# The routed stage, the step sizes and the mixer's first projections put into one block

## The reference, cut to what matters

```python
x = _layernorm(x + _L0_ffn_ref(x, ...))     # routed LoRA: base + top-2 of 8 experts of rank 16
x = _layernorm(x + _L1_attn_ref(x, ...))    # mixer: 8 groups of 16 heads, head size 64, state 128
# inside _L1_attn_ref
proj = jnp.einsum('bsd,ed->bse', x, in_proj_w)          # gate, heads' inputs, B, C and dt
hBC = jax.nn.silu(conv(hBC))                            # causal convolution, 4 taps per channel
dt = jnp.clip(jax.nn.softplus(dt + dt_bias), 0.0, 100.0)
A_dt = dt * A                                           # A = -exp(A_log)
L = jnp.exp(_segsum(A_dt))                              # decay between two tokens of a chunk
Y_diag = einsum(C, B, L, hs * dt)                       # one chunk of 128 tokens is one batch here
g = (Y + hs * D) * silu(gate)                           # then an RMS norm per group, and out_proj
```

## Time and profile before

| | |
|---|---|
| median of 3 runs | 2599.43 us (2597.91 to 2603.35) |
| the profiled execution's own time | 2601.73 us |
| its span | 2600.0 us |
| PE busy | 2485.4 us, 96% |
| DVE busy | 1861.0 us, 72% |
| ACT busy | 1125.2 us, 43% |
| POOL busy | 1077.5 us, 41% |
| mean granted clock of PE | 0.98 |

### The profile page before, as it was taken

How to read it: one execution, slowest core, us unless ns; L and a number is a source line. 1 busy time by engine, 2 the same in 40 slices (tenths; PEclk the granted TensorE clock), 3 DMA queues, 4 the chain that set the end, 5 groups by cost and what they waited for, 6 DMA issues and landing times. The chain is left out here.

```text
span 2600.0 us, 39171 instructions
## 1 busy us (share of the span) xinstructions
PE 2485.4 (96%) x14056; PEld 2038.8 (78%) x14056; DVE 1861.0 (72%) x2531; ACT 1125.2 (43%) x2660; POOL 1077.5 (41%) x889
## 2 busy tenths in 40 slices
PE   7878599999999999999999999989999999999999
PEld 4436488888888888888888888778888888888886
DVE  4865488697786986967859869656666666666675
ACT  2321334334343443343434433445556556565551
POOL 3011264555555546655555556633223223122223
PEclk9988799999999999999999999989999999999999
DMA  4000242131221321313213213111001001010100
GB/s 155 1 1 9 73 145 91 53 146 37 105 102 37 138 89 57 142 37 114 94 48 127 89 61 110 57 37 38 25 17 42 17 25 41 10 33 25 55 3 33
DMA packets 61555, 163.83 MB, mean 63 GB/s; under 512 B 8336, under 2 KB 8976, under 8 KB 52944
## 3 DMA queue, kind: packets, MB, share of 16 engines
q1 hardware_dynamic: 60144, 159.21, 17.8%
q10 hardware_dynamic: 1248, 2.36, 0.3%
HBM read 158.92 MB, written 2.62 MB: 62 GB/s over the span
## 5 line engine op out<-in xcount | busy, mean ns | idle before, releaser
L267 PE MATMUL pair<-XH,d_w_hi 128*128 128x512 f32 x1160 | 475.4, 410 | 29.1 <-POOL d_w_lo L1332 10.4
L268 PE MATMUL pair<-XL,d_w_hi 128*128 128x512 f32 x1160 | 463.0, 399 | 0.0
L269 PE MATMUL pair<-XH,d_w_lo 128*128 128x512 f32 x1160 | 462.4, 399 | 0.0
L1449 DVE TENSOR_TENSOR_SCAN d_decay<-d_decay,m_delta 128x1024 f32<-128x1024 f32 x128 | 359.9, 2813 | 13.7 <-DMA d_decay<-token_decays 12.3
L1351 POOL TENSOR_TENSOR d_decay<-d_decay,d_cb 128x1024 f32<-128x1024 f32 x128 | 309.6, 2419 | 136.4 <-DVE d_decay L1449 125.5
L1332 POOL TENSOR_TENSOR d_w_lo<-d_w,d_w_hi 128x512 fp32r<-128x512 f32 x144 | 187.9, 1308 | 284.2 <-ACT d_w_hi L1214 283.6
L267 PEld LDWEIGHTS pair<-XH,d_w_hi 128*128 128x128 f32 x1160 | 220.8, 190 | 87.9 <-issue 20.7
L1434 DVE SCALAR_TENSOR_TENSOR d_hs<-pair,d_conv,d_hs 128x1016 f32<-128x1016 f32 (+2 forms) x192 | 242.9, 1265 | 33.1 <-ACT d_hs L1239 28.6
L269 PEld LDWEIGHTS pair<-XH,d_w_lo 128*128 128x128 f32 x1160 | 220.4, 190 | 53.7
L268 PEld LDWEIGHTS pair<-XL,d_w_hi 128*128 128x128 f32 x1160 | 221.1, 191 | 47.6
L1356 POOL TENSOR_TENSOR d_gated_lo<-d_gated,d_gated_hi 128x512 fp32r<-128x512 f32 x128 | 173.6, 1359 | 157.4 <-ACT d_gated_hi L1258 157.4
(11 more groups left out here) (280 smaller groups left out, 6032.7 us busy)
## 6 DMA issues: line engine op xcount, KB each, us to landing
d_decay<-token_decays SPq DMA_DIRECT2D x64, 1024.0 KB, 4.9
d_w<-in_L_w_groups SPq DMA_DIRECT2D x144, 256.0 KB, 2.7
e_w<-in_L_w_heads SPq DMA_DIRECT2D x80, 256.0 KB, 2.7
d_wo<-in_L_wo_groups SPq DMA_DIRECT2D x64, 256.0 KB, 5.0
X<-in_x SPq DMA_DIRECT2D x8, 256.0 KB, 10.4
b_ctx<-in_ctx SPq DMA_DIRECT2D x8, 256.0 KB, 11.8
e_ctx<-in_ctx_t SPq DMA_DIRECT2D x4, 512.0 KB, 6.7
out<-X SPq DMA_DIRECT2D x8, 256.0 KB, 2.0
```

The costliest lines, as they stand in the source:

```text
L267: pe.matmul(out, wh, xh, start=first, stop=False)
L268: pe.matmul(out, wh, xl, start=False, stop=False)
L269: return pe.matmul(out, wl, xh, start=False, stop=last)
L1449: v.tensor_tensor_scan(r, r, m["DELTA"][:], 0.0, ALU.mult, ALU.add).then_inc(q["decay"], 1)
```

## The change

The three stages become one block, `stage_routed_mixer`. The operations of the routed stage and of the step sizes become methods of two classes, `RoutedLora` (low, out, turn on PE; exp, mid_turned, hi on ACT; route, sums, lo on DVE) and `TokenSteps`, and are written between the mixer's own. The barrier and clearing between the stages go, and so does the barrier behind the counters' start values: a semaphore `preset` stands for it. The three splits w_lo of the first weights (0, 1, 2) and that of dt's weight stand on POOL between the norms of batches 1 to 5; the latter was on DVE. dt's temporary tiles lie at the place of the mixer's gated and output-weight tiles, the routed small tiles and three tiles of the autocorrelation in the area of the decays, dt's weights in that of the heads. Methods that are not shown here hold the statements of the functions before, word for word but for names.

```diff
+class TokenSteps:
...
+    def inputs(self, sp):
+        q, a = self.q, self.a
+        sp.dma_start(self.W[:], a["L1_w_dt"].rearrange("p (k n) -> p k n", k=KD)).then_inc(q["in_"], 16)
+        sp.dma_start(self.BIAS[:], a["L1_attn_dt_bias"].rearrange("(p o) -> p o", o=1)).then_inc(q["in_"], 16)
+        sp.dma_start(self.A[:], a["L1_attn_A_log"].rearrange("(p o) -> p o", o=1)).then_inc(q["in_"], 16)
+        sp.dma_start(self.m["PAR"][:], a["L1_params"]).then_inc(q["par_in"], 16)
+
+    def store(self, sp):
+        sp.wait_ge(self.q["cut"], 1)
+        sp.dma_start(self.rows, self.N[:]).then_inc(self.q["stored"], 16)
+        sp.wait_ge(self.q["stored"], 16)
+
+    def project(self, pe, h, routed):
+
+        c = self.c
+        if h == 0:
+            pe.wait_ge(self.q["w_lo"], 1)
+        pe.wait_ge(routed.s.summed, NB - 1 + h)
+        pe.wait_ge(routed.s.lo, 4 * h + 4)
...
+    def w_lo(self, pool):
+        pool.wait_ge(self.q["w_hi"], 1)
+        pool.tensor_tensor(self.WL[:], self.W[:], self.WH[:].bitcast(F32), ALU.subtract).then_inc(self.q["w_lo"], 1)
...
+                for handle in q.values():
+                    sp.sem_inc(handle, START)
+                sp.sem_inc(preset, 1)
+                steps.inputs(sp)
                 for i in range(5):
                     weight(0, i)
+                steps.store(sp)
                 decays(0, 0)
...
                     for j in range(JT - 1):
                         project(g, hs_item(j + 1))
                         turn_hs(g, j)
-                        project(g, gate_item(j))
+                        if g or j:
+                            project(g, gate_item(j))
                         scan(g, j)
...
-                project(0, 0)
+                routed.low(pe, 0)
+                for b in range(NB):
+                    if b + 1 < NB:
+                        routed.low(pe, b + 1)
+                    routed.out(pe, b)
+                    if b:
+                        routed.turn(pe, b - 1)
+                pe.wait_ge(preset, 1)
+                steps.project(pe, 0, routed)
+                routed.turn(pe, NB - 1)
+                project(0, 0, (0,))
+                steps.project(pe, 1, routed)
+                project(0, 0, (1,))
                 project(0, 1)
                 project(0, 2)
+                steps.turn(pe)
+                project(0, gate_item(0))
                 cb(0)
...
-                for i in range(3):
-                    w_hi(0, i)
-                evac(0, 0)
+                routed.exp(act, 0)
+                for b in range(NB):
+                    if b + 1 < NB:
+                        routed.exp(act, b + 1)
+                    routed.mid_turned(act, b)
+                    if b:
+                        routed.hi(act, b - 1)
+                    if b == 1:
+                        steps.w_hi(act)
+                        steps.rates(act)
+                        act.wait_ge(preset, 1)
+                    if b in (2, 3, 4):
+                        w_hi(0, b - 2)
+                routed.hi(act, NB - 1)
+                evac(0, 0, (0,))
+                steps.exp(act)
+                evac(0, 0, (1,))
                 w_hi(0, 3)
-                silu(0, 0)
+                steps.log(act)
                 evac(0, 1)
                 w_hi(0, 4)
+                steps.decay(act)
+                evac(0, 2)
+                silu(0, 0)
                 silu(0, 1)
-                evac(0, 2)
                 silu(0, 2)
...
-                for i in range(5):
-                    w_lo(0, i)
+                pool.memset(routed.L[:], NEG).then_inc(routed.q["const"], 1)
+                steps.constants(pool)
+                for b in range(NB):
+                    if b == 2:
+                        steps.w_lo(pool)
+                        pool.wait_ge(preset, 1)
+                    if b in (3, 4, 5):
+                        w_lo(0, b - 3)
+                    norm_rstd(c, pool, routed.s, b)
+                w_lo(0, 3)
+                w_lo(0, 4)
+                steps.cut(pool)
                 scores(0, 0, 0)
                 scores(0, 0, 1)
...
-                tables(0)
-                skip_table(0)
+                v.wait_ge(routed.q["const"], 1)
+                routed.route(v, 0)
+                for b in range(NB):
+                    if b:
+                        norm_apply(c, v, routed.s, b - 1)
+                    if b + 1 < NB:
+                        routed.route(v, b + 1)
+                    routed.sums(v, b)
+                    if b >= 2:
+                        routed.lo(v, b - 2)
+                    if b == 3:
+                        v.wait_ge(preset, 1)
+                        v.wait_ge(steps.q["par_in"], 16)
+                        conv_table(0)
+                        skip_table(0)
+                        v.wait_ge(q["conv_par"], START + 1)
+                norm_apply(c, v, routed.s, NB - 1)
+                routed.lo(v, NB - 2)
+                routed.lo(v, NB - 1)
+                steps.biased(v, 0)
+                conv(0, 0, (0,))
+                steps.biased(v, 1)
+                steps.one(v)
+                conv(0, 0, (1,))
+                steps.rest(v)
+                steps.steps(v)
+                conv(0, 1, (0,))
+                steps.copied(v)
+                conv(0, 1, (1,))
+                v.wait_ge(steps.q["copied"], 2)
+                token_table(0)
+                conv(0, 2)
+                v.wait_ge(steps.q["mask"], 2)
+                cb_mask(0)
+                v.wait_ge(steps.q["delta"], 1)
                 decay(0, 0, 0)
                 decay(0, 0, 1)
-                for i in range(3):
-                    conv(0, i)
-                cb_mask(0)
+                v.wait_ge(q["tok_par"], START + 1)
```

More of the change, by code:

```diff
@@ L730, in routed_weights @@
                 B=sb("c_b", [P, D]), base_t=base_t, router_lora_a=router_lora_a, lora_b=lora_b)
[L733 to L837, removed]
-                                    WD[:, b, :].rearrange("p (e o) -> p e o", o=1).broadcast_to([P, E0, R0]),
-                                    ALU.mult).then_inc(q["mid"], 1)
-                v.wait_ge(q["const"], 1)
-                route(0)
[L842 to L846, removed]
-                    v.wait_ge(q["out_ready"], b + 1)
-                    v.tensor_tensor(c.X[:, b, :], c.X[:, b, :], c.bank[2 + b % 2][:, :], ALU.add).then_inc(s.summed, 1)
-                    norm_moments(c, v, s, b)
-                    if b >= 2:
-                        turned_lo(c, v, s, b - 2, x_bank(b - 2))
-                norm_apply(c, v, s, NB - 1)
-                turned_lo(c, v, s, NB - 2, x_bank(NB - 2))
-                turned_lo(c, v, s, NB - 1, x_bank(NB - 1))
@@ L963, in stage_mixer, with stage_routed_mixer @@
+def stage_routed_mixer(c, w, m, w_groups, wo_groups, rows, e, a, low):
     nc = c.nc
@@ L973, in stage_mixer, with over @@
         BC = R[:, BC_SLOT, :, :]
+        routed = RoutedLora(c, e, w)
+        steps = TokenSteps(c, m, e, low, a, rows.rearrange("g j (e t) -> (g j e) t", e=2))
+        def over(name, shape, words, dt=F32):
+            return nc.alloc_sbuf_tensor_at(name, shape, dt, offset=low + 4 * words)
         XDT = sb("d_xdt", [P, NB, P])
         SQ, SQS = XDT, sb("d_sq_sum", [P, 2, S])
-        GT = sb("d_gated", [P, JT, T])
+        GT = over("d_gated", [P, JT, T], 0)
         GH, GL = sb("d_gated_hi", [P, 2, 4, S], F32R), sb("d_gated_lo", [P, 2, 4, S], F32R)
-        WOR = sb("d_wo", [P, 2, D])
-        WOH, WOL = sb("d_wo_hi", [P, JT, D], F32R), sb("d_wo_lo", [P, JT, D], F32R)
+        WOR = over("d_wo", [P, 2, D], JT * T)
+        WOH, WOL = over("d_wo_hi", [P, JT, D], JT * T + 2 * D, F32R), sb("d_wo_lo", [P, JT, D], F32R)
         DTG = sb("d_dtg", [P, NB, HG])
@@ L1105, in project @@
                         pe.wait_ge(q["tap"], START + 3 * (g * NU + last_unit + 1))
-                    for h in range(2):
+                    for h in halves:
                         for k in range(KD):
```

342 lines of the change are left out of this document (215 added, 127 removed).

## The result

The changed kernel took 2564.43 us (median of 4 runs, 2563.57 to 2565.1) against 2600.49 (4 runs, 2597.91 to 2603.35) of the kernel before, measured beside it: ratio 0.9858, 95% interval 0.9843 to 0.9872. That is 36.1 us less, where 42.7 were forecast; 2564.43 lies 1.4 above the upper end of the range given (2563).

A forecast was written before the change was run, and what follows sets the result against it. PE's waits in the 94 us between routed batches and mixer were taken as where time could be had. Weight 5's projection 45.2 us earlier, less 2.5 clock penalty, gave 42.7 net: median 2599.43 to 2556.7, range 2550 to 2563.

The forecast's parts named there:

- Ahead of 245.07, at nothing: Routed stretch before batch 7's turn: added splits and copies fit idle time and cost nothing; uncovered, 5.2 us.
- rival 3: Routed stretch grows by up to 5.2 us as splits or copies hold a norm, DVE and PE: 2562; chance 0.11.
- The chain from 245.07 to weight 5's projection: From batch 7's turn through dt, taps, scans and xdt: PE may project weight 5 at 290.4, 45.2 us less.
- The clock penalty of 2.5: Projection behind PE's wait for xdt runs at the lower clock, costing 2.5 us, leaving 42.7 net.
- The 12.3 leaves 0.6: PE's waits for dt between routed batches and mixer, 12.3 us before, shrink to some 0.6.
- the 2.82 is filled: PE's wait for the last norm, before batch 7's turn, is filled by dt's first projection half, 2.86 us.
- the 10.4 and the 8.2 go whole: PE's waits for the first split weight, 10.4 us, and for dt's split weight, 8.2, disappear entirely.
- 1.0 for the split of weight 4 beside dt's steps: POOL's split of weight 4 running beside DVE's dt steps lengthens those by 1.0 us, between 0 and 1.3.
- Rival 2: Memory path ends last: decay rows land late, sharing transfers with two weights; some 3 us, 2560; chance 0.12.
- rival 4: First weights not split in time, PE still waits the 10.4 us at B: 2567; chance 0.04.
- From weight 5's projection on, as before: From there PE works without a hole before and after, so the mixer's loop carries the earlier start to the end.
- Rival 5: Slower: the loop becomes DVE's, each of 64 pairs longer; at 0.75 us per pair 2605; chance 0.02.

The follow-up runs named there:

- e1_mid: Changed kernel with each of the four splits on POOL among the routed batches waiting until DVE finished the next batch's routing; 2561.7 us, ratio 0.9854.
- e5_serial: Changed kernel with dt's steps first, then B, C and the heads in the old order, gate in its old place; 2586.15 us, ratio 0.9948.
- e9_layout: Kernel before with only tile places changed: slab reserved from the start, three autocorrelation tiles in it; 2601.02 us, ratio 1.0004.
- e8_before: Kernel before, unchanged, run once more for a second trace; 2601.18 us in its single run.
- e3_normed: Changed kernel with each split among the routed batches waiting only until the norm of the batch before is applied; 2563.33 us.
- e10_order: e1_mid with xdt and the heads' taps issued on DVE ahead of the second pair of scans, first batch; 2559.11 us, ratio 0.9841.
- e7_dt: e1_mid with the split of weight 4 on POOL also waiting for dt; 2563.03 us.
- e11_all: e7_dt with the edit of e10_order; 2560.36 us, ratio 0.9843.

## Why the prediction came out as it did

The direction and the mechanism of the gain held; the saving forecast was 6.6 us too large (42.7 against 36.1), because the step that put the routed stretch at nothing failed, and two smaller terms went the same way. By its own steps, in the profiled executions (42.7 net forecast, 37.3 found, 5.4 to explain):

- *"Ahead of 245.07, at nothing"* is the step that failed: +3.6. The step asked whether POOL had time for the splits, and it had. It didn't ask what DVE does in that same microsecond. Written directly behind `norm_rstd`, a split starts exactly when its own engine's result lets DVE begin the norm. e1_mid shows it: same work, other place, 3.3 back. Of the 3.6, 2.3 are the four waits for c_mid_t. Another 1.1 are products around these waits that no longer overlap: the last one ahead of L786 begins 0.93 to 1.00 us before it instead of 0.23, more than the wait's 0.54 to 0.60 explains, and the one behind L786 0.97 after its start instead of 0.86. The remaining 0.3 lie ahead of the first LoRA product (9.13 us against 8.84) and are in e1_mid too. The sentence under rival 3, that the growth stays below 5.2 if DVE and POOL exclude each other on every split, describes what happened; I gave it 0.11 and left it out of the sum.
- *The chain from 245.07 to weight 5's projection*, 45.3 long forecast, took 45.91, and that it is so close is luck in part, since two errors cancel in it. DVE reached the scans 31.5 us behind the turn instead of 32.4. Then the three scans took 8.78 instead of 7.8: scores and scans excluded each other wholly, not by 0.48 a scan. The first two scans took 2.28 and 2.27, the third, which met the first score, 4.40 (up to 289.99), and the second score, begun at 287.80, was over only at 292.12, though one alone takes 2.36. PE's wait was therefore a single one of 5.18 for the scores, not one of 3.4 for xdt (over at 291.10) and one of 2 for the taps of heads 1.
- *The clock penalty of 2.5*, put on a projection behind a wait of 3.4, was 1.5: it fell on the scan (3.51 instead of 1.97), inside those 45.9, and the projection ran at full speed. Only about 0.8 of it is on the path, since the taps were over at 294.88 and the scan at 295.67. So the stretch is 1.9 better than the sum's net (44.6 against 42.7).
- *"The 12.3 leaves 0.6"*, *"the 2.82 is filled"*, *"the 10.4 and the 8.2 go whole"*, *1.0 for the split of weight 4 beside dt's steps*: right, each by its row above. Decays arrived in time: the store was issued at 272.08, and the scans at 281.21 followed the mask with no wait. Rival 2's memory path did not come up, and rival 4 didn't either. Against the signs named, the stretch up to the last turn (to be as long as before within 1 us) and the number of PE's waits came out wrong.
- *From weight 5's projection on, as before*: +2.6. Of this 1.2 is 0.16 to 0.20 in each of the first seven groups (172.8 us each before, 173.0 after, none of it at 1.2 GHz), in the output projection's products, and it is in every variant of the single block, e5_serial too, but not in e9_layout. Its cause stays open. The other 1.4 is where the 1.2 GHz stretches fall around 1600 to 1700.
- *+1.1 ahead of the routed stage*: not of the change (e8_before).

Sum: 3.6 + 2.6 + 1.1 - 1.9 = 5.4. Rival 5 (a slower loop) has a small true core in the open 1.2. Without the collision the kernel takes 2561.7 (e1_mid), inside the range. The range was too narrow for a sum in which three terms, the collision, the loop and the clock's phase, could all go one way.

## What to carry to other kernels

An engine with idle time is not a free place: ask what the neighbour that it can hold (here VectorE, held by GpSimd) executes in that very microsecond, above all when the work is put right behind the instruction that releases the neighbour. A split that waits for a later signal (2 lines) gave 3.3 us of PE time back. And when instructions of two engines exclude each other, order them by who is waited for: moving two scans behind xdt and the taps gave 2.0.

## What the runs showed of the hardware

- A VectorE TENSOR_SCALAR of 128x512 from SBUF to SBUF, with only one tensor as input, is held by a running GpSimd TENSOR_TENSOR: 0.55 becomes 1.44 to 1.50. Even a 128x2 COPY is (0.16 becomes 1.00), while MAX8 and a 128x1 TENSOR_SCALAR aren't (e3_normed).
- VectorE's scans and GpSimd's products of 128x1024, two SBUF inputs each, took turns: a scan of 2.28 took 4.40 with one score beside it, a score of 2.36 took 4.19 and 4.33. A VectorE TENSOR_TENSOR with one input in PSUM ran beside a score at its usual 1.23.
- Where TensorE's stretches at the granted 1.2 GHz fall moves the start of the routed stage by about 2 us: it was 194.42 in e10_order, 194.73 and 196.34 in the two traces of the kernel before, and up to 196.74 in the variants. The total of the kernel before spread from 2595.62 to 2603.57 in 13 runs. A gain of 1 us on the chain (e7_dt, e11_all) can't be read from the total.
